# Attention b on one Trainium2 core: score matmuls in two halves between the transposes of a pair's two units, and the query spreads one pair later

## The reference

```python
q, k, v = (heads(Wq), heads(Wk), heads(Wv))
att_rel_pos = jnp.einsum('bhsd,pd->bhsp', q, pos_emb_k)
i = jnp.arange(ctx)
att_idxs = jnp.clip(i[None, :] - i[:, None], -R, R - 1) % P
att_pos = jnp.take_along_axis(att_rel_pos, att_idxs[None, None, :, :].astype(jnp.int32), axis=3)
attn_val = jnp.einsum('bhsd,bhtd->bhst', q, k) + att_pos
att = jax.nn.softmax((attn_val + att_pos) * attn_scale, axis=-1)
y = jnp.einsum('bhst,bhtd->bhsd', att, v)
return y.transpose(0, 2, 1, 3).reshape(batch, ctx, emb) @ Wp.T
```

## Time and profile before

| what | value |
|---|---|
| median of 3 runs | 6045.19 us (6037.68 to 6051.18) |
| profiled execution, its own time | 6070.41 us |
| its span | 6068.7 us |
| mean granted TensorE clock | 0.793 |
| attention b, first product to last transpose | 4181.9 to 5213.8 us |
| TensorE busy in the whole span | 5151.8 us (85%) |

### The profile page before, as it was taken

How to read it: one execution, slowest core, us unless ns; L and a number is a source line. 1 busy time by engine, 2 the same in 40 slices (tenths; PEclk the granted TensorE clock), 3 DMA queues, 4 the chain that set the end, 5 groups by cost and what they waited for, 6 DMA issues and landing times. The chain is left out here.

```text
span 6068.7 us, 117568 instructions
## 1 busy us (share of the span) xinstructions
PE 5151.8 (85%) x32766; PEld 3551.2 (59%) x32766; DVE 4485.5 (74%) x15503; ACT 3597.9 (59%) x11201; POOL 1321.9 (22%) x1970
## 2 busy tenths in 40 slices
PE   5687887888788778787886999998999999899998
PEld 3344444444444444444443888886666666688887
DVE  3788888888888788878887788885555555588886
ACT  3577778777777677777776222224667767422222
POOL 1101011111101011101010444443111111244444
PEclk6566667666666666666666999999999999999999
DMA  2000000000000000000000444441000000244444
GB/s 56 1 1 1 1 1 1 1 1 1 1 1 1 1 1 1 1 1 1 1 1 1 85 84 84 84 84 34 11 9 11 11 9 11 45 84 84 84 84 98
DMA packets 199615, 163.32 MB, mean 27 GB/s; under 512 B 47971, under 2 KB 195974, under 8 KB 199046
## 3 DMA queue, kind: packets, MB, share of 16 engines
q1 hardware_dynamic: 199046, 157.32, 12.7%
HBM read 146.52 MB, written 10.49 MB: 26 GB/s over the span
## 5 line engine op out<-in xcount | busy, mean ns | idle before, releaser
L733 ACT ACTIVATE junk<-SS,nt 128x256 bf16<-128x256 f32 x3072 | 1514.0, 497 | 23.8 <-DVE SS L853 17.5
L1192 ACT ACTIVATE f_th<-bank 128x256 f32<-128x256 f32 x1088 | 418.1, 384 | 1147.0 <-PE bank L1123 1147.0
L594 PE MATMUL bank<-ident,prob 128*128 128x128 f32 x2048 | 470.3, 371 | 619.2 <-DVE prob L915 618.6
L1092 POOL TENSOR_TENSOR f_hid<-f_g_m,f_cbs 128x256 f32<-128x256 f32 x1024 | 745.2, 728 | 850.0 <-DVE f_g_m L1337 629.1
L594 PEld LDWEIGHTS bank<-ident,prob 128*128 128x128 f32 x2048 | 301.1, 184 | 930.0 <-DVE prob L915 827.8
L572 PE MATMUL bank<-k,q 8*128 8x256 f32 x2048 | 832.5, 584 | 12.0 <-DVE SS L853 12.0
L605 PE MATMUL bank<-pT,vaug 128*32 128x256 f32 x2048 | 795.3, 531 | 23.9 <-ACT pT L743 23.7
L1122 PE MATMUL bank<-f_xTf,wgT 128*128 128x256 f32 x2176 | 693.0, 400 | 52.9 <-DVE f_g_m L1337 39.5
L1738 DVE TENSOR_REDUCE nmx<-bank 128x2 f32<-128x512 f32 x512 | 329.2, 685 | 477.5 <-PE bank L1510 477.5
L572 PEld LDWEIGHTS bank<-k,q 8*128 8x128 f32 x2048 | 475.7, 277 | 327.5 <-issue 135.9
L1123 PE MATMUL bank<-f_xTf,wuT 128*128 128x256 f32 x2176 | 651.4, 381 | 0.0
(11 more groups left out here) (228 smaller groups left out, 8103.4 us busy)
## 6 DMA issues: line engine op xcount, KB each, us to landing
f_cbs<-f_shares SPq DMA_DIRECT2D x512, 256.0 KB, 5.9
qrow<-q_rows SPq DMA_DIRECT2D x512, 8.0 KB
q_rows<-qTb SPq DMA_DIRECT2D x32, 128.0 KB, 1.7
out_dram<-xres SPq DMA_DIRECT2D x4, 1024.0 KB, 9.3
f_shares<-f_combT SPq DMA_DIRECT2D x64, 32.0 KB, 1.5
px<-pext SPq DMA_DIRECT2D x16, 15.8 KB
nat<-in_L_attn_a_W_qkv_dram SPq DMA_DIRECT2D x3, 64.0 KB
bqk<-in_L_attn_a_b_qkv_dram SPq DMA_DIRECT2D x8, 0.1 KB
```

Source lines behind the costliest of these rows:

```text
L594: last = nc.tensor.transpose(PT[h % 2][:, k * T + i * P:k * T + (i + 1) * P], prob[:, h % 2, i, k * P:(k + 1) * P], ident[:, :])
L733: nc.scalar.activation(junk[:, c % 2, :], SS[:, uu % 4, c, :], ACT.Sign, bias=bias(c), accum_out=acc[:, k, uu % 4, c:c + 1]).then_inc(s["s ...
L1092: pool.tensor_tensor(hid[:, e % NBUF, :], g_m[:, e % NBUF, :], cbs[:, par, e, :], ALU.mult).then_inc(s["hid"], 1)
```

## The change

In every pair that has `products`, TensorE's order was: four transposes of unit 2p, four of unit 2p + 1, 16 products. Now it is: four transposes of unit 2p, 8 products (half i = 0 of both units), four transposes of unit 2p + 1, 8 products (half i = 1). Ahead of the first half stands a wait for the exponentials of unit 2p + 1, whose bank the products overwrite. The waits for `q1` and `qz` in pairs 2 and 6 stand ahead of the pair's transposes. `turned` counts once for each half; nobody waits for it. On VectorE both `by_head` move on by one pair, from behind the reductions of pair 1 to behind those of pair 2, and from pair 4 to pair 5. The tile `nmx` has another name.

```diff
@@ products and batch on TensorE
                 def products(p, par):
 
-                    pe.sem_inc(s["turned"], 1)
                     for i in range(2):
+                        pe.sem_inc(s["turned"], 1)
                         for kind in range(2):
...
                                 if i == 1 and kind == 1:
                                     last.then_inc(s["scores"], 1)
+                        yield
...
                 for p in range(2):
-                    products(p, 0)
+                    for _ in products(p, 0):
+                        pass
...
                     for p in range(PAIRS):
-                        transposes(b, 2 * p)
-                        transposes(b, 2 * p + 1)
+                        rest = iter(())
                         if p + 2 < PAIRS:
                             if p + 2 == PER:
                                 pe.wait_ge(s["q1"], 2 * b + 2)
                                 pe.wait_ge(s["qz"], 2 * b + 2)
-                            products(p + 2, par)
+                            rest = products(p + 2, par)
                         elif more:
                             if p + 2 == PAIRS:
                                 pe.wait_ge(s["q1"], 2 * b + 3)
                                 pe.wait_ge(s["qz"], 2 * b + 3)
-                            products(p + 2 - PAIRS, 1 - par)
+                            rest = products(p + 2 - PAIRS, 1 - par)
+                        transposes(b, 2 * p)
+                        pe.wait_ge(s["exp"], UNITS * b + 2 * p + 2)
+                        next(rest, None)
+                        transposes(b, 2 * p + 1)
+                        next(rest, None)
@@ batch on VectorE
                                 normalise(b - 1, 0, PREV_N0(b))
+                        if p == 2:
                             by_head(b, par, 1)
                         if p == 4:
                             if prev:
                                 normalise(b - 1, 1, use(b, "n1"))
+                        if p == 5:
                             if more:
                                 dve.wait_ge(s["mc"], use(b, "qk'") + 1)
                                 by_head(b + 1, 1 - par, 0)
```

More of the change, by code:

```diff
@@ L1380, in build @@
         rinvb = bb_("rinvb", [P, H])
-        nmx = bb_("nmx", [P, 4, 2])
+        nmx = bb_("nmxb", [P, 4, 2])
         scr = nc.dram_tensor("q_rows", (2, H, HD, J, A), f32, kind="Internal").ap()
```

## The result

The changed kernel takes 6120.34 us (median of 4 runs, 6108.02 to 6134.66), the kernel before 6048.18 (median of 4 runs, 6037.68 to 6058.82). The ratio on record is 1.0124, with a 95% interval from 1.0103 to 1.0145; the two medians alone give 1.0119. Forecast were 6122 us and a ratio of 1.0127. The profiled execution has a span of 6132.9 us, 64.2 more than before.

The account below looks back on a forecast made before the run. TensorE's own stream was taken to bound attention b. 88.9 us for tile changes plus 2 at back edges less 14.4 for the removed wait gave +77, so 6045 + 77 = 6122 us; 8 in 10 from 6098 to 6145.

Parts of the forecast that it names:

- Where the bound is: Attention b ends when TensorE's own stream ends; a change is worth what it alters in that stream's start-to-start distances.
- The price of an excursion, 0.35 us a pair: TensorE going from products into transposes and back once more per pair: 0.35 us in 254 pairs, 88.9 us slower.
- What the split gives, 14.4 us: In pair 3 TensorE's wait for the copy `pTb` goes: 30 times 0.48 us, 14.4 us faster.
- The moved waits and spreads at nothing: Waits for `q1` and `qz` and VectorE's later spreads cost nothing, with 1.9 and 4.8 us of slack, and give nothing.
- new wait for ScalarE: Rival: a new wait on ScalarE or for the later copy, 0.3 to 1 us a batch, adds 10 to 30 us; chance 0.10.
- The back edges, 2 us: At the loop's 14 back edges one exchange may run at 1.2 GHz: at most 5 us slower, 2 taken.
- the sum of 77: Whole kernel: 88.9 + 2 - 14.4 = +77 us.
- The batch of 33.35 us: Sign in attention b's loop: a batch lasts 31.03 + 2.8 - 0.48 = 33.35 us.
- The upper bound of +84: Forecast's bounds: 0.32 to 0.37 us a pair and a 0.3 us wait left or gone give +69 to +84.

Follow-up runs that it names:

- e2: Kernel before with only VectorE's part of the change, both spreads one pair later, TensorE's order as before: ratio 1.0003 to the kernel before.
- e3: Changed kernel with both units' transposes first, then the two product halves back to back with count and wait between: ratio 0.9997 to the kernel before.
- e7: Kernel before with ScalarE's copies of keys, queries and sums in pair 3 taken behind unit 6's exponentials: ratio 1.0016 to the kernel before.
- e12: Kernel before with ScalarE's copies in pair 3 behind unit 6's exponentials, and `weigh` in two runs of 8 steps, not four of 4: ratio 0.9993.
- e4: Changed kernel with quarters instead of halves, two transposes then one group of products, four times a pair: ratio 1.0380 to the kernel before.
- e8: Changed kernel with the split order in pair 3 of each batch alone, spreads as in the changed kernel: ratio 1.0022 to the kernel before.
- e6: Changed kernel with the first half of the products, all eight transposes in one run, then the second half: ratio 1.0152 to the kernel before.
- e1: Changed kernel with VectorE's spreads as before, so TensorE's new order alone: ratio 1.0121 to the kernel before.
- e14: Kernel before with ScalarE's later copies, longer `weigh` runs and attention b's batches written out on TensorE, ScalarE and VectorE: ratio 0.9886 to the kernel before.

## Why the prediction was right

*Where the bound is.* Right: e2 and e3 change VectorE and TensorE's steps and move nothing, and each change of TensorE's start-to-start distances moves the steady batch by as much. The stage follows, except where the back edges take the gain, as they do in e7 and e12.

*The price of an excursion, 0.35 us a pair.* The step was right, its size 0.31, measured in the steady batches of after, e4 and e8. The row that I added from was at fault: the 0.55 us of four transposes in pair 3 stand behind idle time and are 0.53 elsewhere, and the sum for the new order rounded three further distances up by 0.01, that for the old one one. 254 x 0.31 = 78.7 us instead of 88.9. That the price belongs to the excursion and not to its length or its waits is shown by e3, e4 and e6. That it is the draining of the array at a change of tiling mode is the word of the Trainium skill, TensorEngine Tiling (Array Packing), Key Properties. The runs agree with it: the price stands at every change between 64 by 64 tiles and the full array, and there is none between two kinds of full-array steps (0.97 us for eight transposes behind any of them in a steady batch of the kernel before, but for the wait in pair 3). But none of them made transposes on 64 by 64 tiles, so the mode itself was not taken away alone, and that it is a draining is not shown.

*What the split gives, 14.4 us.* Right: the wait is gone in the steady batches of the changed kernel; e7, which takes it away without the split, measures it as 0.50 us against the 0.48 of the sum.

*The moved waits and spreads at nothing.* Right, by e2. No new wait for ScalarE came either: 31.03 - 0.48 + 8 x 0.31 = 33.03 is the whole steady batch.

*The back edges, 2 us.* Too small, and for a reason that I had not named. The excess of an edge rose from 3.01 to 3.44 us, 14 x 0.43 = 6 us. Of these, 0.34 an edge is longer idle time (2.13 to 2.47 on average over the 14), and 7 slow edges instead of 6 make up the rest. The steady part would have given 78.7 - 14.4 = 64 us, and with 6 at the edges it comes to the 70 us by which the stage grew. So two terms were off in opposite directions, by 10 and by 4 us, and it is in part luck that the sum of 77 fell only 5 us from the difference of the medians, 72. The batch of 33.35 us that the prediction named shows the first error by itself: it measured 33.03.

*A slip in the bounds.* The upper bound of +84 does not come out of its own terms: 0.37 us a pair with a wait of 0.3 us left in 30 batches gives 94 + 2 - 14.4 + 9 = +91, without the wait +82. The stated range did not hang on it.

## What to carry to other kernels

On TensorE, count how often a stream goes between full-array steps and small tiles, and price it from start-to-start distances; busy shares showed nothing of it here. Splitting a run to fill a wait pays only where the wait is longer than the excursion (here 0.48 against 0.31 us, in one pair of eight, and even that was not seen in the time). Mending the order of the engine that is late gave more, 0.50 us a batch without an excursion. A gain of tenths of a microsecond a turn has to be checked at the loop's back edge too: there these kernels lose 3.0 to 4.4 us every second batch, more than any of the orders wins in two batches, and writing the batches out is worth 0.9%.

## What the runs showed of the hardware that was not expected

- At a back edge TensorE stands idle for 1.7 to 3.8 us. At most edges the profile names nothing that it waits for, at the others the exponentials, and without the loops that time is gone. What sets its length was not found. The shortest idle of a trace is 2.22 us in both kernels with the changed order (after, e1) and 1.83 to 1.91 in before, e2, e3, e7, e8 and e12, so the order plays a part; but it is not the number of excursions, as e4 has idles from 1.73 us.
- Behind such an idle time the granted clock is sometimes at the 1.2 GHz level for the next rows and sometimes not. In the same trace, changed kernel, TensorE's timeline shows both: idle of 2.26 us with full speed behind it (granted clock 1.00 over the next 2.97 us), and idle of 2.46 us with half (0.50 over the next 2.91 us).

```profile
4766.53 0.65 PE L1497 MATMUL bank<-ident,probb 128*128 128x128 f32 x4 [2.26 <-issue]
```

```profile
4974.39 1.11 PE L1497 MATMUL bank<-ident,probb 128*128 128x128 f32 x4 [2.46 <-issue]
4975.43 1.13 PE L1510 MATMUL bank<-kTb,q 64*64 64x256 f32 x8
```

- How often it happens differs between the kernels (6 to 13 of 14 edges), in a way that none of these runs settles; one profile stands behind each count. That the lost gain of e7 and e12 went to the back edges is shown by their traces and by e14, which keeps it without edges.
